# Second attention of a four-layer kernel: values of a key tile formed in one piece instead of two halves

## Chip, core and metric

The kernel runs on one core of a Trainium2 chip. The metric is the device time of one execution in microseconds (us). Engines are named as the profile names them: PE is TensorE (PEld its weight loads), DVE is VectorE, ACT is ScalarE, POOL is GpSimd, SP is SyncE, which issues most DMAs.

## What is computed

Four layers run one after the other on 8192 tokens of 128 channels (16 sequences of 512): a windowed attention, a routed feed-forward layer, a full attention with 16 heads of 8 channels, and a feed-forward layer. Each is wrapped as `x = x + layernorm(layer(layernorm(x)))`. The change lies in the third, whose core in the reference is:

```python
qkv = x @ Wqkv + bqkv
q = _apply_rope(q, cos, sin)
k = _apply_rope(k, cos, sin)
scores = jnp.einsum('bhqd,bhkd->bhqk', q, k) * scale
attn = jax.nn.softmax(scores, axis=-1)
out = jnp.einsum('bhqk,bhkd->bhqd', attn, v)
return out @ Wout + bout
```

No mask is applied: every query of a sequence meets all 512 keys, in each of 16 heads.

## The kernel before

`l1_attention` (L1356) treats one sequence, called a batch here, in 32 **steps** (STEPS). The 16 heads fall into 4 groups (NG) of 4 heads (GH); a group takes 8 steps (UNITS), two steps for each of its 4 key tiles of 128 keys (NT), one for each pair of heads. The batches overlap: while step n of one batch runs, the first half of the next one is prepared 13 steps ahead (AHEAD). Each engine has its own program with the same steps, written out once for two batches inside a loop over batches 2 to 13 (`turns`); batches 0, 1, 14 and 15 stand outside the loop. Every engine works strictly in the order of its program; semaphores tie them together.

In a step, PE issues in this order:

- `shifted` (L1973): two products `d_t_`, the shifted scores of one key tile for one pair of heads, all 512 queries. They go into three banks `t_ps` in turn, so that step n may start once the first of the two exponentials of step n-1 is done.
- `scores` (L1955): two products `d_s_` of a unit 13 steps ahead. DVE takes the row maximum of both (`maximum`, L1759), ACT does the exponentials of `d_t_` into `pT` (L1688).
- what `SLOTS` puts there: the turning in of the normalised tokens (`turn_in`, L1909, step 22 of 32), the four projections of queries and keys (`q0` to `q3`, L1916, steps 23, 24, 26 and 27), the values (`v`, L1921, step 9), the turning out of a finished group (`out0` to `out3`, L1928), `att` (L1935, step 9) and `y` (L1942, step 12). All of them, and `scores`, share the two banks `s_ps` in turn: before each, `room` waits until DVE or ACT has read what stood two places earlier in that order.
- `weighted` (L1986): the product of `pT` of one key tile with the values `v`, added up in the bank `o_ps` (32 partitions for each of the 4 heads, 512 queries) over the four key tiles of a group. Where it stands is told by the table `VALUES`: step within the group's count, key tile, and the halves of the 512 queries.

When a group's last product is done, ACT copies `o_ps` out (L1707, step 10 counted from the group's first), behind its exponentials of that step. The three bf16 parts of queries and keys are made by ACT (L1718, L1722) and POOL and are put into `qs` and `ks` by DMAs that SP issues (L1577). The row maxima go in by four further DMAs for each group (L1585), on the same queue, behind the former where both are due; the first `d_t_` of a group waits for them.

All values are f32 here; a matmul of f32 operands goes to PE as two passes, each an instruction of its own in the trace. The four heads of a product sit on four different column groups of 32 and their passes run side by side, so that 8 instructions (4 heads, 2 passes) form one half of a key tile.

Of the kernel before, what the change touches and what calls it, by code (L numbers as in the profile page):

```python
# [1355 lines left out]
def l1_attention(nc, x, pos, sorted_rows, mean, rstd, wqk_d, wv_d, bqk_d, bv_d, wo_d, bo_d, rope_d, ident_in):  # L1356
# [10 lines left out]
    NT = 4  # L1367
    T = NT * 128
# [4 lines left out]
    GH = 4  # L1373
    NG = H // GH
    HC = 32
# [15 lines left out]
    STACK = {-32: (0, 0, (0, 1, 2)), -31: (1, 0, (0, 3)), -27: (1, 0, (5,)), -26: (0, 1, (3, 4)), -25: (1, 1, (1, 4)),  # L1391
             -24: (0, 2, (5,)), -23: (1, 2, (2,))}
    SHIFTS = -4
    VALUES = ((4, 0, (0, 1)), (5, 1, (0,)), (6, 1, (1,)), (7, 2, (0,)), (8, 2, (1,)), (9, 3, (0,)), (10, 3, (1,)))
    COPY_OUT = 10
    PLUS, ATT = 38, 39
    STAT_Y, STAT_Y2, ROOT_Y, NORM_Y, NORM_Y2, ADD_Y = 47, 48, 51, 60, 62, 63
# [2 lines left out]
    with ExitStack() as ctx:  # L1400
        def sb(name, shape, dt=F32):
            return ctx.enter_context(nc.sbuf_tensor("d_" + name + "_", shape, dt))
# [24 lines left out]
        v = [sb(f"v{k}", [128, NT, H, HC]) for k in range(2)]  # L1427
        nmax = [sb(f"nmax{k}", [128, 32], BF16) for k in range(2)]
        nmaxT = [sb(f"nmaxT{k}", [128, 32], BF16) for k in range(2)]
        pT = [[sb(f"pT{k}_{r}", [128, 2, T]) for r in range(2)] for k in range(NT)]  # L1430
# [24 lines left out]
        o_ps = ps("o", [128, T])  # L1455
# [23 lines left out]
        av_done = sem("av_done")  # L1479
# [43 lines left out]
        for s in range(STAT_IN, STEPS * NB + LAST + 1):  # L1523
            turn = Turn(s // STEPS, 0, 0)
            unit = (s + AHEAD) % STEPS
            for what, at in [(unit, unit - AHEAD)] + [(w, SLOT_STEP[w]) for w in slots_of(s % STEPS)]:
                e = of(turn, s % STEPS, at)
# [21 lines left out]
        def dve_read(what, e):  # L1549

            return counted(what, e, "dve")
# [341 lines left out]
        def _(pe):  # L1893
# [79 lines left out]
                    nc.tensor.matmul(t_ps[(2 * n + a + e.k) % 3][:], ks[e.k][rows, hp, kt * 128:(kt + 1) * 128],  # L1973
                                     qs[e.k][rows, hp, :], start=True, stop=True).then_inc(st_done, 1)

            def weighted(e, g, kt, halves):
                pe.wait_ge(exp_done, 2 * STEPS * e.n + 2 * UNITS * g + 4 * kt + 4)
                if kt == 0:
                    if g == 0:
                        pe.wait_ge(read_dve, dve_read("v", e))  # L1980
                    if not (isinstance(e.n, int) and e.n == 0 and g == 0):
                        pe.wait_ge(oe_done, NG * e.n + g)
                for half in halves:
                    cols = slice(half * T // 2, (half + 1) * T // 2)
                    for i in range(GH):
                        ins = nc.tensor.matmul(o_ps[HC * i:HC * (i + 1), cols], v[e.k][:, kt, g * GH + i, :],  # L1986
                                               pT[kt][i // 2][:, i % 2, cols], start=(kt, half) == (0, 0),
                                               stop=(kt, half) == (NT - 1, 1), skip_group_check=True)
                if halves[-1] == 1:
                    ins.then_inc(av_done, 1)  # L1990

            def step(turn, n):
                e = of(turn, n, n)
                if e is not None:
                    shifted(e, n)
                unit = (n + AHEAD) % STEPS
                e = of(turn, n, unit - AHEAD)
                if e is not None:
                    scores(e, unit)
                for what in slots_of(n):  # L2000
                    e = of(turn, n, SLOT_STEP[what])
                    if e is None:
                        continue
                    room(what, e)
                    if what == "turn_in":
                        turn_in(e)
                    if what[0] == "q":
                        project(e, int(what[1]))
                    if what == "v":
                        project_v(e)  # L2010
                    if what[0:3] == "out":
                        turn_out(e, int(what[3]))
                    if what == "att":
                        turn_attention(e)
                    if what == "y":
                        project_out(e)
                for g in range(NG):
                    for at, kt, halves in VALUES:
                        e = of(turn, n, UNITS * g + at)
                        if e is not None:  # L2020
                            weighted(e, g, kt, halves)

            pe.wait_ge(loaded, 16 * NLOADS)
            pe.wait_ge(const_set, 8)
# [497 lines left out]
```

## Time and profile before

| | us |
|---|---|
| median of 3 runs | 2857.4 |
| lowest and highest run | 2855.66, 2862.07 |
| the profiled execution, device time | 2855.56 |
| its span (first to last instruction) | 2853.8 |
| second attention: first and last `d_t_` of L1973 | 1720.0 to 2644.8 |

The span is 1.8 us shorter than the device time of the same execution. The page of the profile cuts the span into 40 slices of 71 us; the second attention fills slices 25 to 37. In it 512 steps take 925 us, 1.81 us each, and a batch takes 51 to 62 us.

### The profile page before, as it was taken

The page shows a single profiled execution, that of the slowest core. Times are in us where ns is not written, and L with a number is a line of the kernel's source. Part 1 is how long each engine was busy: PE and PEld are TensorE (multiplying, and loading weights), DVE is VectorE, ACT ScalarE, POOL GpSimd, SP SyncE. Part 2 cuts the span into 40 slices and gives each one's busy share as a digit, 9 for nine tenths or more (in the row PEclk, how much of TensorE's full clock was granted, in tenths as well). Part 3 has the DMA queues.
Part 4 walks back from the last instruction along what each step waited for, and adds up shares of the span by engine and source line. Part 5 has one row for each costly group of instructions (what it writes and reads, how often), then busy time and mean ns, then how long its engine had stood idle before and what let it go on. Part 6 is the DMA issues. An engine that isn't in the chain of part 4 may idle for free. (4 is left out here: it accounts for less than half of the span.)

```text
span 2853.8 us, 73730 instructions
## 1 busy us (share of the span) xinstructions
PE 2106.2 (74%) x26748; PEld 1206.3 (42%) x26748; DVE 2078.9 (73%) x5353; ACT 1500.5 (53%) x2776; POOL 1161.3 (41%) x1165
## 2 busy tenths in 40 slices
PE   4898989888989987111009828888888888888597
PEld 3676767666767766100004302222322222232354
DVE  4677777776767775766417828888888888888598
ACT  4565656565656652000005406666666666667487
POOL 5677667676767770000363346311221112210122
PEclk9999999999999996555559958998999999999799
DMA  3233333332333330000022233311122111120001
GB/s 103 65 82 72 73 75 74 79 77 70 74 75 76 75 70 6 1 1 1 21 69 68 77 64 59 51 27 24 24 30 37 28 24 23 29 39 4 9 26 33
DMA packets 103685, 136.76 MB, mean 48 GB/s; under 512 B 23782, under 2 KB 78982, under 8 KB 103047
## 3 DMA queue, kind: packets, MB, share of 16 engines
q1 hardware_dynamic: 99206, 123.34, 19.6%
q0 software_dynamic: 4096, 8.40, 1.1%
q8 instruction: 232, 3.80, 0.6%
q14 instruction: 151, 1.23, 0.2%
HBM read 26.52 MB, written 12.58 MB: 14 GB/s over the span
## 5 line engine op out<-in xcount | busy, mean ns | idle before, releaser
L1759 DVE TENSOR_REDUCE d_nmax_<-d_s_ 128x2 bf16<-128x1024 f32 x512 | 619.9, 1223 | 116.3 <-PE d_s_ L1955 113.7
L1688 ACT ACTIVATE d_pT_<-d_t_ 128x512 f32<-128x512 f32 x1024 | 557.1, 598 | 243.7 <-PE d_t_ L1973 235.7
L303 POOL TENSOR_TENSOR a_other<-a_other,a_rope 128x512 f32<-128x512 f32 x256 | 322.1, 1279 | 300.6 <-DMA a_other<-a_raw 300.4
L1986 PE MATMUL d_o_<-d_pT_,d_v_ 128*32 128x256 f32 x4096 | 332.3, 410 | 0.2 <-ACT d_pT_ L1688 0.2
L1973 PE MATMUL d_t_<-d_qs_,d_ks_ 49*128 49x512 bf16 x1024 | 207.5, 402 | 84.2 <-ACT d_pT_ L1688 42.4
L371 ACT ACTIVATE a_pT<-a_t 64x384 f32<-64x384 f32 x512 | 248.2, 485 | 33.2 <-PE a_t L621 23.9
L509 DVE RECIPROCAL a_rden<-a_o 128x512 f32<-128x512 f32 x64 | 214.5, 3352 | 52.7 <-PE a_o L634 52.7
L1955 PE MATMUL d_s_<-d_ks_,d_qs_ 48*128 48x512 bf16 x1024 | 208.0, 403 | 58.3 <-DMA d_ks_<-d_part_ 29.0
L477 DVE TENSOR_TENSOR a_qT<-a_proj,a_rope 128x512 f32<-128x512 f32 x128 | 87.6, 684 | 165.4 <-ACT a_raw L352 165.3
L1188 ACT ACTIVATE c_hT_<-c_in_,c_beta_,c_gamma_ 128x512 f32<-128x512 f32 x16 | 12.4, 777 | 359.2 <-PE c_in_ L1308 359.2
L823 POOL DMA_INDIRECT sorted_x<-x_tokens,pos x64 | 61.5, 961 | 313.8 <-DVEq L720 294.6
L352 ACT COPY a_raw<-a_proj 128x512 f32<-128x512 f32 x256 | 150.6, 588 | 73.4 <-PE a_proj L540 68.7
L540 PE MATMUL a_proj<-a_xnT_hi,a_w_lo 128*128 128x512 f32 x256 | 116.8, 456 | 93.9 <-ACT a_v L334 88.0
L1973 PEld LDWEIGHTS d_t_<-d_qs_,d_ks_ 49*128 49x128 bf16 x1024 | 49.7, 93 | 316.4 <-ACT d_pT_ L1688 203.5
L358 ACT CAST a_qB<-a_qT 128x512 bf16<-128x512 f32 x128 | 79.3, 620 | 184.9 <-POOL a_qT L308 184.8
L877 PE MATMUL b_tot<-b_count,b_ones 128*128 128x3 bf16 x126 | 23.6, 187 | 201.1 <-DVE b_junk L959 189.3
L643 PE MATMUL a_o<-a_pT,a_v 128*32 128x160 f32 (+1 forms) x4096 | 168.4, 306 | 4.1 <-DVE a_oT L514 2.4
L308 POOL TENSOR_TENSOR a_kT<-a_kT,a_other 128x512 f32<-128x512 f32 x128 | 164.1, 1282 | 0.0
L308 POOL TENSOR_TENSOR a_qT<-a_qT,a_other 128x512 f32<-128x512 f32 x128 | 163.6, 1278 | 0.0
L1986 PEld LDWEIGHTS d_o_<-d_pT_,d_v_ 128*32 128x32 f32 x4096 | 90.5, 111 | 172.6 <-ACT d_pT_ L1688 90.9
L548 PE MATMUL a_y<-a_wo,a_oT 128*128 128x128 f32 x1024 | 135.2, 287 | 17.2 <-issue 16.4
L643 PEld LDWEIGHTS a_o<-a_pT,a_v 128*32 128x32 f32 x4096 | 123.9, 113 | 37.1 <-issue 21.4
(269 smaller groups left out, 4695.6 us busy)
## 6 DMA issues: line engine op xcount, KB each, us to landing
a_other<-a_raw SPq DMA_DIRECT2D x512, 128.0 KB, 2.4
d_qs_<-d_part_ SPq DMA_DIRECT2D x192, 64.0 KB
d_ks_<-d_part_ SPq DMA_DIRECT2D x192, 64.0 KB
a_xpre<-x SPq DMA_DIRECT2D x16, 256.0 KB, 2.8
a_xres<-x SPq DMA_DIRECT2D x16, 256.0 KB, 2.9
c_xs_<-sorted_x SPq DMA_DIRECT2D x16, 256.0 KB, 2.7
c_w_<-e_w SPq DMA_DIRECT2D x16, 256.0 KB, 3.2
sorted_x<-c_xs_ SPq DMA_DIRECT2D x16, 256.0 KB, 2.0
```

The costliest lines, as they stand in the source:

```text
L303: nc.gpsimd.tensor_tensor(other[s % 2][:, side, :], other[s % 2][:, side, :], rope[:, 1, :], ALU.mult).then_inc(rope2_done, 1)
L308: nc.gpsimd.tensor_tensor(dst, dst, other[s % 2][:, side, :], ALU.add).then_inc(add_done, 1)
L352: nc.scalar.copy(raw[s % 2][:, side, :], proj[bank][:, 0:T]).then_inc(copied, 1)
L371: nc.scalar.activation(dst[rows, :, 64 * c:64 * c + HB], src[rows], ACT.Exp, scale=SCALE).then_inc(exp_done, 1)
L509: nc.vector.reciprocal(rden[:], o_ps[:, 0:T]).then_inc(rden_done, 1)
L548: ins = nc.tensor.matmul(y_ps[:, t * 128:(t + 1) * 128], oT[:, 2 * (chunk % 2) + half, t * 128:(t + 1) * 128], wo_sb[:, 2 * chunk + half, ...
L643: ins = nc.tensor.matmul(o_ps[QD * i:QD * (i + 1), 128 * t:128 * t + widths[t]], v_sb[k_v][:, t, col:col + QD], pT[k_p][i][:, BAND * t:BAN ...
L1688: nc.scalar.activation(pT[kt][pair][:, a, :], t_ps[(j + turn.k) % 3][:], ACT.Exp).then_inc(exp_done, 1)
L1759: nc.vector.reduce_max(out, bank_of(unit, e)[:], AX_X, negate=True).then_inc(read_dve, 1)
L1955: nc.tensor.matmul(bank_of(unit, e)[:, a, :], qs[e.k][rows, hp, qt * 128:(qt + 1) * 128], ks[e.k][rows, hp, :], start=True, stop=True).the ...
L1973: nc.tensor.matmul(t_ps[(2 * n + a + e.k) % 3][:], ks[e.k][rows, hp, kt * 128:(kt + 1) * 128], qs[e.k][rows, hp, :], start=True, stop=True ...
L1986: ins = nc.tensor.matmul(o_ps[HC * i:HC * (i + 1), cols], v[e.k][:, kt, g * GH + i, :], pT[kt][i // 2][:, i % 2, cols], start=(kt, half) = ...
```

## The change

The table `VALUES` loses its halves. Before, key tile 0 of a group stood whole in step 4 (both halves, one behind the other), and the two halves of tiles 1, 2 and 3 stood in steps 5 and 6, 7 and 8, 9 and 10. Now tile 0 stands in step 4, tile 1 in step 6, tile 2 in step 8, tile 3 in step 10, each as one product of all 512 queries. `weighted` issues 8 instructions of 512 columns for a key tile where it issued 16 of 256. In the numbering of a batch's 32 steps every even step now has a whole tile and no odd step has any, where before steps 4, 12, 20 and 28 had a whole tile, steps 3, 11, 19 and 27 none, and all others a half.

```diff
-    VALUES = ((4, 0, (0, 1)), (5, 1, (0,)), (6, 1, (1,)), (7, 2, (0,)), (8, 2, (1,)), (9, 3, (0,)), (10, 3, (1,)))
+    VALUES = ((4, 0), (6, 1), (8, 2), (10, 3))
...
-            def weighted(e, g, kt, halves):
+            def weighted(e, g, kt):
...
-                for half in halves:
-                    cols = slice(half * T // 2, (half + 1) * T // 2)
-                    for i in range(GH):
-                        ins = nc.tensor.matmul(o_ps[HC * i:HC * (i + 1), cols], v[e.k][:, kt, g * GH + i, :],
-                                               pT[kt][i // 2][:, i % 2, cols], start=(kt, half) == (0, 0),
-                                               stop=(kt, half) == (NT - 1, 1), skip_group_check=True)
-                if halves[-1] == 1:
-                    ins.then_inc(av_done, 1)
+                for i in range(GH):
+                    ins = nc.tensor.matmul(o_ps[HC * i:HC * (i + 1), :], v[e.k][:, kt, g * GH + i, :],
+                                           pT[kt][i // 2][:, i % 2, :], start=kt == 0, stop=kt == NT - 1)
+                ins.then_inc(av_done, 1)
...
-                    for at, kt, halves in VALUES:
+                    for at, kt in VALUES:
                         e = of(turn, n, UNITS * g + at)
                         if e is not None:
-                            weighted(e, g, kt, halves)
+                            weighted(e, g, kt)
```

The order of PE at the projections, before (from `q0` of step 23 to the values of step 24; in these listings a matmul is one call, so `x2` is two heads; L1973 opens a step). This is the loop's first batch:

```order
L1916 MATMUL d_s_<-d_zT_,d_wqk_ 128x512
L1977 REGISTER_ALU
L1986 MATMUL d_o_<-d_pT_0_,d_v_ 32x256 x2
L1986 MATMUL d_o_<-d_pT_1_,d_v_ 32x256 x2
L1965 REGISTER_ALU
L1973 MATMUL d_t_<-d_qs_,d_ks_ 128x512 x2
L1904 REGISTER_ALU
L1955 MATMUL d_s_<-d_ks_,d_qs_ 128x512 x2
L1904 REGISTER_ALU
L1916 MATMUL d_s_<-d_zT_,d_wqk_ 128x512
L1986 MATMUL d_o_<-d_pT_0_,d_v_ 32x256 x2
L1986 MATMUL d_o_<-d_pT_1_,d_v_ 32x256 x2
```

The same place with the change:

```order
L1916 MATMUL d_s_<-d_zT_,d_wqk_ 128x512
L1965 REGISTER_ALU
L1973 MATMUL d_t_<-d_qs_,d_ks_ 128x512 x2
L1904 REGISTER_ALU
L1955 MATMUL d_s_<-d_ks_,d_qs_ 128x512 x2
L1904 REGISTER_ALU
L1916 MATMUL d_s_<-d_zT_,d_wqk_ 128x512
L1977 REGISTER_ALU
L1984 MATMUL d_o_<-d_pT_0_,d_v_ 32x512 x2
L1984 MATMUL d_o_<-d_pT_1_,d_v_ 32x512 x2
```

Step 23 has lost its half, and step 24 has both halves of the tile in one piece, still behind the projection `q1`.

The order of PE at step 9, with `v` and `att`, and step 10, before:

```order
L1921 MATMUL d_s_<-d_wv_,d_zT_ 128x128 x4
L1904 REGISTER_ALU
L1935 MATMUL d_s_<-d_ident_,d_att_ 128x128 x4
L1977 REGISTER_ALU
L1986 MATMUL d_o_<-d_pT_0_,d_v_ 32x256 x2
L1986 MATMUL d_o_<-d_pT_1_,d_v_ 32x256 x2
L1965 REGISTER_ALU
L1973 MATMUL d_t_<-d_qs_,d_ks_ 128x512 x2
L1904 REGISTER_ALU
L1955 MATMUL d_s_<-d_ks_,d_qs_ 128x512 x2
L1986 MATMUL d_o_<-d_pT_0_,d_v_ 32x256 x2
L1986 MATMUL d_o_<-d_pT_1_,d_v_ 32x256 x2
```

The same place with the change:

```order
L1921 MATMUL d_s_<-d_wv_,d_zT_ 128x128 x4
L1904 REGISTER_ALU
L1935 MATMUL d_s_<-d_ident_,d_att_ 128x128 x4
L1965 REGISTER_ALU
L1973 MATMUL d_t_<-d_qs_,d_ks_ 128x512 x2
L1904 REGISTER_ALU
L1955 MATMUL d_s_<-d_ks_,d_qs_ 128x512 x2
L1977 REGISTER_ALU
L1984 MATMUL d_o_<-d_pT_0_,d_v_ 32x512 x2
L1984 MATMUL d_o_<-d_pT_1_,d_v_ 32x512 x2
```

Here nothing stands between `att` and the next step's `d_t_` and `d_s_` any more; the whole tile has gone behind them.

## Rows read from the trace of the kernel before

**Rows 1.** Page, busy tenths of DVE in 40 slices of 71 us
```profile
DVE  4677777776767775766417828888888888888598
```

**Rows 2.** Windows, whole second attention: window, length, busy us (instructions) by engine, clock
```profile
1720.00:2647.00 927.00, 778.20 (x6836) 265.03 (x6840) 797.18 (x1370) 626.39 (x1175) 211.82 (x194) 0.94 0.19 31
```

**Rows 3.** Waits, 1720 to 2647: engine line, releaser: us, times, longest
```profile
DVE d_nmax_ L1759 <- PE d_s_ L1955: 100.4, 129, 4.4
```

**Rows 4.** Timeline: start, us, engine line op xcount; a half, then a whole tile
```profile
2012.29 0.39 PE L1973 MATMUL d_t_<-d_qs_,d_ks_ 49*128 49x512 bf16 x2
2012.51 0.38 PE L1955 MATMUL d_s_<-d_ks_,d_qs_ 48*128 48x512 bf16 x2
...
2012.71 1.08 ACT L1688 ACTIVATE d_pT_<-d_t_ 128x512 f32<-128x512 f32 x2 [0.63 <-PE d_t_ L1973]
2012.82 0.16 PEld L1986 LDWEIGHTS d_o_<-d_pT_,d_v_ 128*32 128x32 f32 x8 [0.43 <-issue]
2012.82 0.64 PE L1986 MATMUL d_o_<-d_pT_,d_v_ 128*32 128x256 f32 x8
...
2013.39 0.39 PE L1973 MATMUL d_t_<-d_qs_,d_ks_ 49*128 49x512 bf16 x2
...
2081.63 1.07 PE L1986 MATMUL d_o_<-d_pT_,d_v_ 128*32 128x256 f32 x16
...
2082.63 0.39 PE L1973 MATMUL d_t_<-d_qs_,d_ks_ 49*128 49x512 bf16 x2
```

**Rows 5.** Timeline, steps 11 and 12 of batch 6: exponentials and the step they release
```profile
2094.24 2.19 ACT L1688 ACTIVATE d_pT_<-d_t_ 128x512 f32<-128x512 f32 x4
...
2094.92 0.39 PE L1973 MATMUL d_t_<-d_qs_,d_ks_ 49*128 49x512 bf16 x2 [0.83 <-ACT d_pT_ L1688]
```

**Rows 6.** Timeline, steps 22 to 27 of batch 7, PE and DVE
```profile
2173.87 0.65 PE L1909 MATMUL d_s_<-d_ident_,d_zz_ 128*128 128x128 f32 x4 [0.17 <-DVE d_quot_ L1792]
...
2175.02 0.39 PE L1973 MATMUL d_t_<-d_qs_,d_ks_ 49*128 49x512 bf16 x2
...
2175.70 1.23 DVE L1759 TENSOR_REDUCE d_nmax_<-d_s_ 128x2 bf16<-128x1024 f32 x1 [0.69 <-PE d_s_ L1955]
...
2176.84 0.74 DVE L1771 SCALAR_TENSOR_TENSOR d_prod_<-d_s_,d_bqk_,d_rope_ 128x512 f32<-128x512 f32 x1
...
2177.72 1.13 PE L1916 MATMUL d_s_<-d_zT_,d_wqk_ 128*128 128x512 f32 x2
...
2179.35 0.39 PE L1973 MATMUL d_t_<-d_qs_,d_ks_ 49*128 49x512 bf16 x2
...
2180.46 0.39 PE L1973 MATMUL d_t_<-d_qs_,d_ks_ 49*128 49x512 bf16 x2
...
2181.31 1.13 PE L1916 MATMUL d_s_<-d_zT_,d_wqk_ 128*128 128x512 f32 x2 [0.24 <-DVE d_nmax_ L1759]
...
2182.94 0.39 PE L1973 MATMUL d_t_<-d_qs_,d_ks_ 49*128 49x512 bf16 x2
```

**Rows 7.** Timeline, steps 9 and 10 of batch 6, PE and DVE
```profile
2089.70 1.16 PE L1921 MATMUL d_s_<-d_wv_,d_zT_ 128*128 128x128 f32 x8 [1.23 <-DVE d_nmax_ L1759]
...
2091.80 0.64 PE L1986 MATMUL d_o_<-d_pT_,d_v_ 128*32 128x256 f32 x8
...
2093.05 1.23 DVE L1759 TENSOR_REDUCE d_nmax_<-d_s_ 128x2 bf16<-128x1024 f32 x1 [1.30 <-PE d_s_ L1955]
```

**Rows 8.** Timeline, batch 7: DMAs of the maxima, and the step 8 that waits
```profile
2140.48 2.23 SPq L1585 DMA_DIRECT2D d_qs_<-d_nmaxT_  x4
...
2147.00 0.39 PE L1973 MATMUL d_t_<-d_qs_,d_ks_ 49*128 49x512 bf16 x2 [2.92 <-DMA d_qs_<-d_nmaxT_]
```

**Rows 9.** Timeline of PE, steps 0 and 1 of batch 6, after the loop's turn
```profile
2073.80 0.61 PE L1973 MATMUL d_t_<-d_qs_,d_ks_ 49*128 49x512 bf16 x2 [2.43 <-issue]
...
2075.77 0.61 PE L1973 MATMUL d_t_<-d_qs_,d_ks_ 49*128 49x512 bf16 x2
```

**Rows 10.** Windows, batch 6, steps 0 to 2: columns as in Rows 2, clock 0.50
```profile
2073.80:2079.70 5.90, 5.90 (x36) 1.07 (x36) 3.31 (x3) 3.76 (x7) 1.62 (x2) 0.50 0.48 85
```

## The prediction

> **What bounds the kernel now.** I began with the page's 40 slices: the second attention is the long stretch of eights on the vector engine from slice 25 on [rows 1]. The windows give it 797 us of work on the vector engine in 927, against 778 on PE and 626 on ACT [rows 2]. No engine is full. The vector engine has least room, 1.56 us of work in a step of 1.81, and what it waits for is nearly all one thing: the scores of L1955, 100 us in 129 waits [rows 3]. So a change on PE is worth what it does to the time at which `d_s_` comes in those steps where DVE has nothing else. Time saved where DVE is behind is worth nothing, and time added where PE leads DVE costs the full amount. The timeline of single steps, not the sums, decides this.
>
> **Prices of the pieces.** In a step, `d_s_` starts 0.22 us after `d_t_`, the values 0.31 after `d_s_`, and the next `d_t_` 0.57 after a half tile: 1.10 us together [rows 4]. A whole tile in 16 instructions takes 1.00 to the next `d_t_` [rows 4].
>
> The 512-column form in four column groups is not in the trace. Lower bound: the streaming is the same number of columns and each half shows two sets of four passes, so at best only the starts of two sets are saved; I take 0.98. Upper bound: the two passes of `q1`, 512 columns of f32 on all 128 columns with its own weight loads, whose record lasts 1.13 [rows 6] and which holds the next piece off for 1.06 (2179.35 is 1.63 after it starts, less the half's 0.57). I keep 0.98 because the rows of the same product are nearer, and 1.06 for the range.
>
> So a split tile cost 2 x (0.57 + 0.09) = 1.32 us (0.09 is how much later something starts behind `d_s_` when it is the values than when it is the next `d_t_`, 0.31 less 0.22) and a whole one costs 0.98 + 0.09 = 1.07. That is 0.25 saved for each of 3 x 64 = 192 split tiles, 48 us of PE time, and 0.02 for the 64 whole ones, 1 us. What matters is where it lies: an odd step loses 0.57, an even step gains 0.41.
>
> The trace shows all eight weight loads of a half inside 0.16 us while its first passes run [rows 4]. The Trainium skill ("TensorE: Matmul & The Clock Gate", Measured speedup vs the span model) says that weight loads overlap running matmuls only where the row group differs; here all use all 128 rows, so by it each set would stand still for its load, and longer products would save more. The row shows the overlap, and I do not add to the 0.25. The skill's page "TensorEngine Tiling (Array Packing)" (Key Properties) states that changing the tiling mode drains the engine. It speaks for fewer changes between values and scores; what such a change costs is already inside the rows' 0.31 and 0.57, and by it the forecast would stay as it is.
>
> **Light steps do not hand on what they save.** A step may open when the first exponential of the step before is done. The next `d_t_` starts 0.68 after that exponential [rows 5], and an exponential starts 0.42 after its `d_t_` when ACT is idle [rows 4], so two steps lie at least 1.10 us apart however little PE has to do. Before, a pair of steps took 2.2 us on PE and on this chain alike. After, the heavy step takes 0.22 + 0.31 + 0.98 = 1.51 and the light one still 1.10: 2.61. Unless a light step holds other PE work (a slot), its saving is lost, and the 0.41 stays.
>
> **Where DVE covers it: nothing.** In steps 13 to 21 and 4 to 8 the reductions run one behind the other with statistics, quotients and normalisation between them, at 1.5 to 1.7 us a step, and PE waits for room in `s_ps`. Pairs of 2.61 fit below that. If this cover is gone (a stretch where DVE needs less than 1.3 us a step), each pair there costs 0.4.
>
> **Steps 22 to 27, the projections.** Here PE holds most work and DVE waits for it. `turn_in` of step 22 is pinned by DVE's quotients (0.17 wait at 2173.87), so what step 21 saves before it is lost. Then, with [rows 6]:
> - step 22 has the whole tile: step 23 opens at 2173.87 + 0.58 + 0.98 = 2175.43, not 2175.02: +0.41.
> - step 23, light, has `q0`: step 24 opens at 2175.43 + 0.54 + 1.06 = 2177.03, not 2177.18. But the reduction of step 23 is late by 0.41 as well: 2176.11, and the first `d_prod_` follows 1.14 later as before, 2177.25 to 2177.99.
> - step 24: `q1` needs the bank of `q0`, so it waits for that `d_prod_`: 2178.1 where PE would be ready at 2177.57. Step 25 opens at 2178.1 + 1.06 + 0.98 = 2180.13, not 2179.35: +0.78.
> - step 25, light: 1.10 before and after, by the exponential. +0.78 stays.
> - step 26: `q2` waits for the reduction of step 25 as now (0.24), which is late by the same 0.78, then the whole tile: +0.41. Step 27 opens 1.2 late. Steps 27 and 28 are unchanged.
>
> The pattern of these six steps is the same in all batches that have projections, 0 to 13: 14 x 1.2 = **+16.8 us**. From step 28 on DVE is the bound, and carries the delay on.
>
> **Steps 8 to 10.** In step 9, `v` and `att` wait for DVE, and then the half stands before the scores that DVE lacks (1.30 us idle) [rows 7]. It goes: 0.57 earlier. In the five batches that open the loop again this is a full gain, 5 x -0.58 = -2.9. In the nine batches whose step 8 waits for DMAs [rows 8] step 8 starts at the landing and is 0.41 heavier first; where `v` then waits for the vector engine anyway the net is -0.5, where not -0.16. I take -0.35: -3.1. Together **-6.0 us**.
>
> **Steps 30 and 31 and the DMAs behind them.** The scores of step 30 are pinned by DVE, the whole tile behind them makes step 31 and the casts on ACT 0.41 late, and SP's chain of transfers, whose last four carry the maxima of the next group, starts that much later. In nine batches PE's step 8 waits for just these four (2.92 us idle at 2147.00, landing 6.5 after the first issue at 2140.48) [rows 8]. 9 x 0.41 = **+3.7**. Whatever steps 0 to 7 of these batches gain or lose is swallowed by that wait. Where the loop turns, five times, PE stands still about 2.4 us for nothing that the profile shows [rows 9]; the last half before it is gone: 5 x (0.41 - 0.57) = **-0.8**.
>
> **Steps 0 to 3 after the loop's turn.** At the upper clock level steps 0 to 2 go from 1.1 + 1.1 + 1.46 to 1.51 + 1.10 + 1.51, of which DVE feels 0.3. At the lower level of 1.2 GHz (granted clock 0.50 [rows 10]) a step with a half takes 1.97 [rows 9]; a whole tile adds 0.85 (two more sets at twice 0.21), a light step takes 1.33: 2.82 + 1.33 + 2.82 against 5.9, +1.06. Five turns at a mean of 0.7: **+3.5**.
>
> **The last two batches.** There DVE has little to do, and pairs go from 2.2 to 2.6 in some eight pairs: **+3.0**.
>
> **Sum**: 16.8 - 6.0 + 3.7 - 0.8 + 3.5 + 3.0 = +20.2. The profiled execution took 2855.6, so 2875.8; its median is 1.8 higher. I predict 2876.
>
> **Rivals.**
> 1. *PE's saving is on the path.* If light steps are not held by the exponential, or `q1` finds its bank free, the 48 us that PE saves count where DVE waits for it. For: DVE's wait of 100 us is on PE alone. Against: behind a step with no values at all PE still waits 0.83 us for ACT [rows 5]. Half of the 48 us, since DVE is the bound in about half of the steps: 2855.6 - 24 = 2832. It decides as soon as the six projection steps come out shorter than before.
> 2. *All absorbed.* The +0.41 of each heavy step stays within what DVE has queued, also at the projections, and the landing of the maxima is set by something else: only -6 and +6 of small terms, 2857. For: DVE is busy 86%. Against: its 0.69 idle at 2175.70 means that nothing is queued there.
> 3. *More time at the lower clock.* PE works 49 us less and in clumps. The granted clock in the stage is 0.94 [rows 2], and it was at the lower of its two levels behind a stop of 2.4 us [rows 9, 10]. If half of the 64 groups got one heavy step at the lower level (+0.85) and a third of that reached DVE, +9; with 1.06 instead of 0.98 for a whole tile, +0.08 x 3 x 14 = +3.4, and with all turns of the loop slow +1.8: 2890. The Trainium skill ("TensorE: Matmul & The Clock Gate", Why this matters for your kernels) warns of idle gaps between bursts of matmuls, which is the direction of this rival; no row here prices it for light steps.
> 4. *The change is not what it says.* The instruction order shows 8 calls of 32x512 where 16 of 32x256 stood, so no chance is given.
>
> **How the numbers follow.** Forecast 0.6, own range 2864 to 2888; rival 1 0.16; rival 2 0.12; rival 3 0.12. The range reaches over rival 2 and 3 and leaves out most of rival 1: 2853 to 2895. About 0.2% (6 us) is what a measurement of this kernel tells from no change, so "same" is 2852 to 2863. Faster: rival 1, 0.16. Same: rival 2 and a sliver of the forecast, 0.14. Slower 0.70.
>
> **What would show it.** Right: steps 22 to 27 longer by 1.2 us in every batch, with a wait of `q1` for `d_prod_` of about 0.5 that was not there; light steps 1.10 apart; DVE's wait for L1955 up by 10 to 20 us from 100; step 10's reduction 0.5 earlier. PE's busy time down by some 30 to 50 us. Wrong: light steps shorter than 1.0, or whole tiles of more than 1.1 us at the upper clock level, or a time that differs outside 1720 to 2647.

## The result, and the profile after

| | before | after |
|---|---|---|
| median, us | 2859.74 | 2869.62 |
| lowest and highest | 2853.06, 2862.80 | 2864.93, 2872.48 |
| ratio, 95% interval | | 1.0035 [1.0019, 1.0051] |
| profiled execution: device time | 2855.56 | 2868.84 |
| its span | 2853.8 | 2867.0 |
| second attention, first to last `d_t_` | 924.4 | 932.0 |

The change makes the kernel slower by 9.9 us, where 16 to 19 were forecast (2876 beside medians of 2857 to 2860). The two profiled executions differ by more, 13.3 us. The second attention holds 7.6 of that. 8.1 us had already gathered by the end of the first attention, whose code is the same, and the stages between and behind gave 2.4 of them back. The experiments come back to it.

The page after. Each line of engines has busy us, share, instructions; the groups have busy us and mean ns of one, then the idle time before them:

```profile
PE 2069.4 (72%) x24700; PEld 1152.6 (40%) x24700; DVE 2081.6 (73%) x5353; ACT 1501.0 (52%) x2776; POOL 1160.9 (40%) x1165
...
DVE  4677777776767775777417828888898888988598
...
q8 instruction: 176, 2.88, 0.4%
...
L1759 DVE TENSOR_REDUCE d_nmax_<-d_s_ 128x2 bf16<-128x1024 f32 x512 | 621.5, 1224 | 122.4 <-PE d_s_ L1955 105.9
...
L1984 PE MATMUL d_o_<-d_pT_,d_v_ 128*32 128x512 f32 x2048 | 282.3, 624 | 0.2 <-ACT d_pT_ L1688 0.2
```

The vector engine's row is that of [rows 1] but for single tenths. PE's total was 2106.2 before: the change does save 37 us of PE. The window of the whole stage, which answers to [rows 2], and three waits in it, which answer to [rows 3]:

```profile
1727.00:2663.00 936.00, 734.15 (x4792) 205.71 (x4792) 799.51 (x1371) 627.67 (x1176) 211.29 (x194) 0.96 0.19 29
```

```profile
DVE d_nmax_ L1759 <- PE d_s_ L1955: 92.9, 107, 2.4
...
DVE d_nmax_ L1759 <- issue: 13.4, 7, 4.4
...
ACT d_oE_ L1707 <- PE d_o_ L1984: 30.3, 38, 1.6
```

PE is busy 44 us less in the stage, and the granted clock went up from 0.94 to 0.96, which rival 3 had the other way round. The vector engine waits for `d_s_` 7.5 us less, not 10 to 20 more. The other two waits grew: the reductions' idle time for which no releaser is shown (`issue`) from 0.3 us to 13.4, and ACT's copy of `o_ps` out from 21.3 to 30.3.

**Where the time went.** Both traces have 512 reductions L1759 in the same order, so each can be set against its partner. This table adds up by how much the second kernel falls behind (+) or gains (-) between the reductions of two steps. It is worked out from the two timelines, batches 0 to 13 together, with the forecast's terms beside it:

| reductions, step to step | after less before, us | forecast |
|---|---|---|
| 31 to 0 (loop's turn) | -2.1 | -0.8 |
| 0 to 4 | -3.7 (five batches behind the turn: -7.8) | +3.5 |
| 4 to 7 | +2.2 | 0 |
| 7 to 9 | +11.5 | +3.7, and part of -6.0 |
| 9 to 10 | -12.0 | rest of -6.0 |
| 12 to 13 | -6.2 (the same five batches: -6.3) | 0 |
| 10 to 12 and 13 to 21 | -1.2 | 0 |
| 21 to 27 (projections) | **+16.7** | **+16.8** |
| 27 to 31 | -0.7 | 0 |
| batches 14 and 15, all steps | +2.0 | +3.0 |
| sum | +6.5 | +26.2 - 6.0 = +20.2 |

Read by batch (from step 31 of the batch before to its own step 31), the same comparison says where the cost stays. Batches 0 to 3 fall behind by 5.3 us and 14 and 15 by 2.4, while the ten batches 4 to 13 come out even (-0.4). There each batch that follows a turn of the loop gains 1.2 to 3.4 us, and its successor loses 1.5 to 3.3. The second execution of the changed kernel, set against the same one of before, gives +7.9, +3.7 and -0.2. So the projections' 1.2 us is paid in every batch, but inside the loop something else pays it back.

### The profile page after: what moved, and what is told of

Read it like the earlier page. It is cut to its first block and busy times, and to the rows that moved or that the text cites. A ratio compares the mean times of both kernels' runs of the same rounds, so it can differ in the third digit from the quotient of the medians.

```text
span 2867.0 us, 69628 instructions
## 1 busy us (share of the span) xinstructions
PE 2069.4 (72%) x24700; PEld 1152.6 (40%) x24700; DVE 2081.6 (73%) x5353; ACT 1501.0 (52%) x2776; POOL 1160.9 (40%) x1165
## 5 line engine op out<-in xcount | busy, mean ns | idle before, releaser
L1759 DVE TENSOR_REDUCE d_nmax_<-d_s_ 128x2 bf16<-128x1024 f32 x512 | 621.5, 1224 | 122.4 <-PE d_s_ L1955 105.9
L1973 PE MATMUL d_t_<-d_qs_,d_ks_ 49*128 49x512 bf16 x1024 | 205.3, 397 | 112.6 <-ACT d_pT_ L1688 84.0
L1984 PE MATMUL d_o_<-d_pT_,d_v_ 128*32 128x512 f32 x2048 | 282.3, 624 | 0.2 <-ACT d_pT_ L1688 0.2
L1973 PEld LDWEIGHTS d_t_<-d_qs_,d_ks_ 49*128 49x128 bf16 x1024 | 49.6, 93 | 443.9 <-ACT d_pT_ L1688 317.0
L548 PEld LDWEIGHTS a_y<-a_wo,a_oT 128*128 128x128 f32 x1024 | 125.8, 200 | 31.7 <-issue 30.6
```

The costliest lines, as they stand in the source:

```text
L548: ins = nc.tensor.matmul(y_ps[:, t * 128:(t + 1) * 128], oT[:, 2 * (chunk % 2) + half, t * 128:(t + 1) * 128], wo_sb[:, 2 * chunk + half, ...
L1759: nc.vector.reduce_max(out, bank_of(unit, e)[:], AX_X, negate=True).then_inc(read_dve, 1)
L1984: ins = nc.tensor.matmul(o_ps[HC * i:HC * (i + 1), :], v[e.k][:, kt, g * GH + i, :], pT[kt][i // 2][:, i % 2, :], start=kt == 0, stop=kt = ...
```

## The projections as the forecast has them

The timeline of batch 7, steps 22 to 27, answers to [rows 6]: start, us, engine, line, operation, and the idle time before it in brackets.

```profile
2184.61 0.65 PE L1909 MATMUL d_s_<-d_ident_,d_zz_ 128*128 128x128 f32 x4 [0.17 <-DVE d_quot_ L1792]
...
2186.19 0.39 PE L1973 MATMUL d_t_<-d_qs_,d_ks_ 49*128 49x512 bf16 x2
...
2187.79 0.39 PE L1973 MATMUL d_t_<-d_qs_,d_ks_ 49*128 49x512 bf16 x2
...
2188.80 1.12 PE L1916 MATMUL d_s_<-d_zT_,d_wqk_ 128*128 128x512 f32 x2 [0.26 <-DVE d_prod_ L1771]
...
2190.86 0.39 PE L1973 MATMUL d_t_<-d_qs_,d_ks_ 49*128 49x512 bf16 x2
...
2191.93 0.39 PE L1973 MATMUL d_t_<-d_qs_,d_ks_ 49*128 49x512 bf16 x2 [0.47 <-ACT d_pT_ L1688]
...
2193.88 1.06 PE L1984 MATMUL d_o_<-d_pT_,d_v_ 128*32 128x512 f32 x8
...
2194.87 0.39 PE L1973 MATMUL d_t_<-d_qs_,d_ks_ 49*128 49x512 bf16 x2
```

From `turn_in` to the opening of step 27 it is 10.26 us, where it was 9.07: +1.19. The wait of `q1` for `d_prod_` that was forecast as about 0.5 is there (0.26 on PE, and its weights waited 0.56). A whole tile holds the next `d_t_` off for 0.99 to 1.00 (2193.88 to 2194.87), where 0.98 was taken. The light step 25 is 1.07 long and PE waits for ACT at its end, where 1.10 was taken.

## Is the 13 us between the profiled executions all the change's?

```diff
(no edit: the kernel before, and the changed kernel, once more)
```

> The kernel before, profiled once more. The changed kernel's profile began its second attention 7.3 us later than the profile of before, in code that neither differs in. Theory A (that is drift between executions): here the first attention, which ended at 1103 us in the profile of before and at 1111 us in that of the change, ends anywhere between these two, and the stretch of the second attention from the first to the last shifted scores takes 925 us within 1 us. Theory B (the changed kernel's code slows the first stages too): the first attention ends at 1103 within 1 us.

> The changed kernel, profiled once more. Theory A (drift): the first attention ends more than 1 us away from the 1111 us of the first profile, and the second attention has again a length 7 to 8 us above that of before. Theory B (its code): the first attention ends at 1111 within 1 us.

The kernel before took 2860.03, the changed one 2871.53. The first attention ended at 1103.0 and 1108.6 us in two executions of the kernel before, and at 1111.1 and 1103.9 in two of the changed kernel. So this unchanged stretch moves by up to 8.1 us from one execution to the next, in both kernels. The theory that the change's shorter code shifts it falls. In the second attention the lengths are 924.4 and 925.0 before, 932.0 and 937.5 after, so the second profile of the changed kernel is 12.5 us above before, not the 7 to 8 that theory A named with the drift. The medians, +9.9, lie between the two.

Paired with the first execution of before as in the table above, its second gave +0.6 in all and a third, on a further chip (below), +0.4. Single cells moved by more: 12 to 13 by +3.0 and +1.3, 9 to 10 by +0.8 and -2.1, 0 to 4 by -2.1 and +0.8, 21 to 27 by 0.0 and +1.1. The two executions of the changed kernel differ by 4.1 in all, 3.1 of it between steps 13 and 21 of batch 0. That is the noise of these tables: a cell of 3 us tells nothing alone, the +16.7, +11.5, -12.0 and -6.2 are clear of it.

## Place or form: two halves behind each other in the changed places

```diff
-    VALUES = ((4, 0, (0, 1)), (5, 1, (0,)), (6, 1, (1,)), (7, 2, (0,)), ...
+    VALUES = (((4, 0, (0, 1)), (6, 1, (0, 1)), (8, 2, (0, 1)), (10, 3, (0, 1))), ...   # in all four groups
```

> Whole tiles in steps 4, 6, 8 and 10 as in the change, but each still as two halves of 256 queries one behind the other: placement without the new form, and as many instructions of PE as before. Theory A (a whole tile costs 0.02 less than two halves; the branch of PE's program at the loop's turn took 3.5 us before and 0.2 after because the loop's code became shorter): the branch takes 3.5 us again at all five turns, steps behind the turn are at the lower clock level again, and the time is 5 to 15 us above that of the change, some 15 to 25 above before, which is what the blind sum of 20 had assumed. Theory B (the short branch came from where PE stands when it branches, not from the length of its code): the branch stays short and the time is that of the change within 4 us.

Measured: 2889.1 (2880.3 to 2898.2), ratio 1.0097 [1.0065, 1.0129], 29 us beside a kernel before of 2860.0. The projections' steps 24 to 27 lose 16 us here as in the changed kernel, and steps 9 to 13 gain the same. What is new lies at the loop's turn: in the five batches behind it 8.9 us between steps 31 and 0 and 5.4 between 0 and 4, where the changed kernel gains. So the *place* costs, and the *form* of 512 columns gives back some 19 us by the medians (26 in the two profiled executions, of which this kernel's was the slowest of its four), most of it at the turn. The branch is long as theory A has it, but longer than its 3.5 us, and the time lies above its 5 to 15. The trace says where: PE's branch at the turn (L1501) takes 3.4 to 4.0 us before, 4.8 to 5.4 here and 0.2 in the changed kernel. It is short in every kernel here with 176 or 178 packets of instructions on queue 8, and long in every one with 226 or 232. The traces show that these go together. They don't show how the length of the code would make the branch long. The timeline of PE in this kernel shows what stands behind the branch in one turn:

```profile
2091.85 0.61 PE L1979 MATMUL d_t_<-d_qs_,d_ks_ 49*128 49x512 bf16 x2 [4.31 <-issue]
...
2094.68 0.61 PE L1979 MATMUL d_t_<-d_qs_,d_ks_ 49*128 49x512 bf16 x2
```

It stands still for 4.31 us, then runs step 0 at the lower clock level, 2.83 us long. And the changed kernel, one batch pair:

```profile
2084.70 0.39 PE L1973 MATMUL d_t_<-d_qs_,d_ks_ 49*128 49x512 bf16 x2 [0.96 <-ACT d_pT_ L1688]
...
2086.81 1.23 DVE L1759 TENSOR_REDUCE d_nmax_<-d_s_ 128x2 bf16<-128x1024 f32 x1 [1.66 <-issue]
```

```profile
2084.70:2089.40 4.70, 3.84 (x28) 0.81 (x28) 3.04 (x4) 4.08 (x8) 2.23 (x2) 1.00 0.30 57
```

PE waits 0.96, for ACT, where [rows 9] had 2.43 for nothing shown, and goes on at a granted clock of 1.00, where [rows 10] had 0.50. But the vector engine has a turn of its own, 1.66 us of nothing, and now it is the one that comes last: of the 1.5 us that PE gains, the reductions gain 0.4 at the turn itself. The larger gain is the clock's, -7.8 in steps 0 to 4 where +3.5 was forecast.

## The projections, from both sides

Group 2 alone back in halves (steps 20 to 26 as before), all else as in the change:

```diff
-        ((4, 0, WHOLE_TILE), (6, 1, WHOLE_TILE), (8, 2, WHOLE_TILE), (10, 3, WHOLE_TILE)),   # group 2
+        ((4, 0, (0, 1)), (5, 1, (0,)), (6, 1, (1,)), (7, 2, (0,)), (8, 2, (1,)), (9, 3, (0,)), (10, 3, (1,))),
```

> The change, but group 2 (steps 20 to 26, where the four projections stand) has its halves in the old places. Theory A (the steps 22 to 27 cost 1.2 us in each of 14 batches and that is carried on): 16 to 17 us below the change, 2853 beside 2870 and 2860, faster than before by 5 to 8 us. Theory B (the delay at the projections is given back at the next wait for a DMA or at the loop's turn): less than 8 us below the change.

Measured: 2865.8, ratio 1.0018 [1.0000, 1.0036] to a kernel before of 2860.0: 6 us below the one execution of the changed kernel on that chip, not 17. That is theory B's size, and its interval overlaps the changed kernel's. In the trace the projection steps 24 to 27 stand at 0.0 in all batches, so the local price is confirmed in full. But 6.1 us have come between steps 27 and 31 (4.9 of them in the odd batches 5 to 13), 3.1 between 21 and 24, and the gain in steps 0 to 4 behind the turn is 4.7 instead of 7.8.

The opposite kernel, halves everywhere and group 2 alone whole:

```diff
-        ((4, 0, (0, 1)), (5, 1, (0,)), (6, 1, (1,)), (7, 2, (0,)), (8, 2, (1,)), (9, 3, (0,)), (10, 3, (1,))),   # group 2
+        ((4, 0, WHOLE_TILE), (6, 1, WHOLE_TILE), (8, 2, WHOLE_TILE), (10, 3, WHOLE_TILE)),
```

> The kernel before, with group 2 alone (steps 20, 22, 24 and 26) in whole tiles; groups 0, 1 and 3 keep their halves. Theory A (the projection steps 22 to 27 cost 1.2 us a batch wherever the rest of the table stands): 14 x 1.2 = 16.8 us more than the kernel before, 2877, and the reductions between step 21 and step 27 late by 1.2 us in every batch from 0 to 13. Theory B (vector engine or clock give it back, as when group 2 alone was put back into halves and only some 5 us of the change's time went): 5 us, 2865. If PE's branch at the loop's turn is short here, some 2 us less in either case; if it is long, the loop's code still counts as long.

It ran on a chip on which the kernel before took 2903.3: there the first two batches lose some 35 us in each of the four kernels traced, with two stops of ACT of 10 to 17 us and shorter ones of the vector engine of up to 14. Only ratios and batches 4 to 13 are used from it. Measured: 2922.4, ratio 1.0073 [1.0050, 1.0096], +19.1 us. In the ten batches 4 to 13 steps 24 to 27 lose 11.3 us, 1.13 each, and 21 to 24 another 3.1. Theory A: here almost nothing gives it back (+13.4 in all over these batches).

Then the same four tiles whole, but not behind `q1` and `q2`:

```diff
-        ((4, 0, WHOLE_TILE), (6, 1, WHOLE_TILE), (8, 2, WHOLE_TILE), (10, 3, WHOLE_TILE)),   # group 2
+        ((4, 0, WHOLE_TILE), (5, 1, WHOLE_TILE), (7, 2, WHOLE_TILE), (9, 3, WHOLE_TILE)),
```

> The kernel before, with group 2 alone in whole tiles, but at steps 20, 21, 23 and 25: none in the steps 22, 24 and 26. Theory A (it is the place of the whole tile that costs: behind q0, q1 and q2 in step 24 and 26): steps 22, 24 and 26 are lighter by a half each, q1 finds its bank free, and steps 22 to 27 become shorter by about 0.9 us in each of 14 batches: 12.5 us below the kernel before, 2847. Theory B (whole tiles cost at the projections wherever they stand, since a pair of steps gets 2.61 instead of 2.2 us): as group 2 whole in even steps, 2865 to 2877.

Measured on the same chip: 2911.6, ratio 1.0024 [1.0007, 1.0040], +8.3. The move is worth 10.8 us against group 2 whole in the even steps, and in batches 4 to 13 the traces put 11.9 of it into steps 21 to 27. The time itself lies at the lower edge of theory B's range (ratio 1.002 to 1.006), so neither theory holds as it stands: the place counts, but a whole tile costs at the new place too. My working of -12.5 against the kernel before was wrong: steps 24 to 27 do gain (0.39 a batch), but the whole tile of step 21 costs 0.63 between 21 and 24 first.

## Step 8, and the clock behind a stop

The changed kernel, batch 7, from the last `d_t_` ahead of the wait for the maxima's DMAs on; it answers to [rows 8]:

```profile
2152.94 0.39 PE L1973 MATMUL d_t_<-d_qs_,d_ks_ 49*128 49x512 bf16 x2
...
2156.75 0.61 PE L1973 MATMUL d_t_<-d_qs_,d_ks_ 49*128 49x512 bf16 x2 [3.20 <-DMA d_qs_<-d_nmaxT_]
...
2157.72 1.93 PE L1984 MATMUL d_o_<-d_pT_,d_v_ 128*32 128x512 f32 x8
...
2159.58 0.61 PE L1973 MATMUL d_t_<-d_qs_,d_ks_ 49*128 49x512 bf16 x2
...
2160.68 1.23 DVE L1759 TENSOR_REDUCE d_nmax_<-d_s_ 128x2 bf16<-128x1024 f32 x1 [1.21 <-PE d_s_ L1955]
```

The windows of what follows the stop (the column ahead of the DMA share is the granted clock), after:

```profile
2156.70:2163.10 6.40, 6.35 (x30) 2.93 (x30) 3.29 (x5) 2.17 (x4) 0.00 (x0) 0.54 0.51 102
```

and in the kernel before, whose step 8 was over in 1.11 us:

```profile
2147.00:2152.30 5.30, 5.30 (x36) 3.17 (x36) 3.46 (x5) 2.61 (x5) 0.00 (x0) 0.68 0.51 103
```

The stop is 0.3 us longer than before (3.20 and 2.92), and behind it the whole step 8 runs at the lower level of 1.2 GHz. It takes 2.83 us, where 1.51 was priced. The vector engine has nothing else and waits 1.21 us for the scores of step 9. Its reductions are late by 0.5 at step 8 and by a further 1.3 at step 9. Of these the 0.5 answers to the forecast's 0.41 for the landing, the 1.3 to a term that I had at 0.41 and then netted away. To see whether it is this tile in this place:

```diff
-        ((4, 0, WHOLE_TILE), (6, 1, WHOLE_TILE), (8, 2, WHOLE_TILE), (10, 3, WHOLE_TILE)),   # group 0
+        ((4, 0, WHOLE_TILE), (6, 1, WHOLE_TILE), (7, 2, WHOLE_TILE), (10, 3, WHOLE_TILE)),
```

> The changed kernel, with tile 2 of group 0 alone moved from step 8 to step 7, ahead of the wait for the maxima's DMAs. Theory A (the whole tile behind that stop is run at the lower clock level and costs 0.9 to 1.4 us in each of nine batches, since nothing but PE holds the vector engine there): 9 to 12 us below the change, 2859 to 2862, step 8 about 1.1 to 1.3 us long instead of 2.8, step 7 longer inside the wait. Theory B (the vector engine has enough queued after the stop, or v waits for it anyway): within 3 us of the change, 2868 to 2874.

Measured: 2905.2, ratio 1.0008 [0.9995, 1.0020], so 8 us below the change by the ratios, the two on different chips, where theory A had 9 to 12 and theory B 3 at most. The same step 8 there:

```profile
2195.28 1.06 PE L1991 MATMUL d_o_<-d_pT_,d_v_ 128*32 128x512 f32 x8
...
2198.26 0.39 PE L1979 MATMUL d_t_<-d_qs_,d_ks_ 49*128 49x512 bf16 x2 [1.91 <-DMA d_qs_<-d_nmaxT_]
...
2199.33 0.39 PE L1979 MATMUL d_t_<-d_qs_,d_ks_ 49*128 49x512 bf16 x2 [0.46 <-ACT d_pT_ L1694]
```

```profile
2198.20:2203.80 5.60, 4.44 (x32) 2.05 (x32) 4.14 (x6) 3.54 (x7) 0.00 (x0) 1.00 0.47 104
```

The tile is done inside the wait, the stop shrinks to 1.91, step 8 takes 1.07 at a granted clock of 1.00. Batch 7 is the best case. In batches 9, 11 and 13 step 8 is at the upper level too, but step 9 has a mean granted clock of 0.62 to 0.65, and in batch 5 both steps are at 0.50. Even so the light step 8 takes only 1.29 there, so most of the gain comes from the tile being gone and not from a better clock.

In the five odd batches 5 to 13 steps 7 to 9 lose 0.3 us instead of 8.8. That is theory A in its place, and the largest single thing that the forecast had left out. Here too something comes back: 5.8 us between steps 21 and 24 of those batches (0.3 in the change). Over batches 4 to 13 this trace is only 2.1 us ahead of the change's, so the 8 us of the ratios are not found in full.

## What gives part of each gain back

A last pair of single edits, with a trace of the kernel before from the same chip:

> The kernel before once more, for a trace of it from the chip on which the next three run. On another chip the whole of it took 2903 us instead of 2857 to 2860, and the readings of three variants put 34 to 36 us of that into steps 4 to 8 of the first batches (0 and 1). If this chip is like that one, these steps are some 34 us longer here too, which is then the chip's and not the edit's; if it is like the first, the second attention takes 924 to 926 us.

It took 2860.23, with a second attention of 924.8 us like that of the first trace: the 35 us of the other chip are that chip's.

```diff
-        ((4, 0, (0, 1)), (5, 1, (0,)), (6, 1, (1,)), (7, 2, (0,)), (8, 2, (1,)), (9, 3, (0,)), (10, 3, (1,))),   # group 0 of before
+        ((4, 0, WHOLE_TILE), (6, 1, WHOLE_TILE), (7, 2, WHOLE_TILE), (10, 3, WHOLE_TILE)),
```

> The kernel before, with group 0 alone in whole tiles, at steps 4, 6, 7 and 10 (none in step 8, which may wait for DMAs, and none in step 9, behind att). Theory A (a half behind att in step 9 delays the scores of step 10 by 0.57 in nearly all batches): step 10's reduction 0.6 to 0.8 earlier in 14 batches, -8 to -11, and nothing at step 12, whose 1.26 us in five batches belongs to group 1: 0.3 to 0.4% below the kernel before. Theory B (the gain at step 12 comes with it, since PE is then at the upper clock level when step 12 begins): -14 to -17, 0.5 to 0.6% below. PE's branch at the loop's turn long, 3.4 to 3.9 us, in both.

Measured: 2846.5, ratio 0.9951 [0.9934, 0.9968], 12.7 us faster. Against the trace of before from the same chip, steps 9 to 10 gain 7.4 us and step 12 another 7.4 (9.4 and 6.1 against the first trace). So the gain at step 12 comes with it as in theory B, whose total of 14 to 17 is not reached. In the kernel before PE is at the lower level in part of step 12 in four or five of the five batches behind a turn, in each of its three traces, after group 0's change in none. The window of step 12 of batch 6, before:

```profile
2095.40:2100.30 4.90, 3.96 (x28) 2.14 (x28) 3.13 (x5) 1.03 (x2) 0.86 (x1) 0.65 0.14 17
```

The branch is long, 3.3 to 3.9 us. 9.2 us come back between steps 21 and 24 of batches 1, 5, 11 and 13. The profiled execution is the slowest of the eight, 2858.1, and its second attention only 2.8 us shorter than that of before. So the trace shows where gains and losses lie, and not how the other executions come to 12.7.

```diff
-        ((4, 0, WHOLE_TILE), (6, 1, WHOLE_TILE), (8, 2, WHOLE_TILE), (10, 3, WHOLE_TILE)),   # group 2 of the change
+        ((4, 0, WHOLE_TILE), (5, 1, WHOLE_TILE), (7, 2, WHOLE_TILE), (9, 3, WHOLE_TILE)),
```

> The changed kernel, with group 2 alone at steps 20, 21, 23 and 25 instead of 20, 22, 24 and 26. Theory A (whole tiles behind q1 and q2 are what costs at the projections, and their place alone mends it): steps 21 to 27 about 1.1 us shorter in each of 14 batches, 15 us below the change, some 5 us below the kernel before (ratio 0.998). Theory B (as with group 2 alone put back into halves, most of the local gain is given back elsewhere): 6 us below the change, ratio 1.002.

Measured: 2863.4, ratio 1.0022 [1.0009, 1.0035]: theory B. Its interval overlaps the change's, so that it is faster at all isn't settled. In the trace, again of the slowest of its executions, steps 24 to 27 are 21 us better than in the change, and 27 to 31 are 9.8 worse, 21 to 24 4.9, 0 to 4 behind the turn 3.4, and the whole stage is 2.3 us longer than in the first trace of the change. The place is step 30, batch 5. First this kernel (L1979 is `shifted`, L1991 `weighted`):

```profile
2079.32 0.39 PE L1961 MATMUL d_s_<-d_ks_,d_qs_ 48*128 48x512 bf16 x2 [1.54 <-DVE d_nmax_ L1765]
...
2079.64 1.80 PE L1991 MATMUL d_o_<-d_pT_,d_v_ 128*32 128x512 f32 x8
...
2081.38 0.61 PE L1979 MATMUL d_t_<-d_qs_,d_ks_ 49*128 49x512 bf16 x2
...
2084.12 1.93 PE L1991 MATMUL d_o_<-d_pT_,d_v_ 128*32 128x512 f32 x8
```

```profile
2077.38:2081.30 3.92, 2.38 (x13) 0.35 (x12) 3.85 (x7) 1.97 (x4) 1.81 (x2) 0.81 0.00 0
2081.37:2085.90 4.53, 3.78 (x20) 0.54 (x16) 1.65 (x3) 2.67 (x5) 1.16 (x1) 0.50 0.09 23
```

and the changed kernel:

```profile
2081.82 0.39 PE L1955 MATMUL d_s_<-d_ks_,d_qs_ 48*128 48x512 bf16 x2 [1.50 <-DVE d_nmax_ L1759]
...
2082.14 1.06 PE L1984 MATMUL d_o_<-d_pT_,d_v_ 128*32 128x512 f32 x8
...
2083.14 0.39 PE L1973 MATMUL d_t_<-d_qs_,d_ks_ 49*128 49x512 bf16 x2
```

```profile
2079.92:2083.10 3.18, 1.68 (x13) 0.35 (x12) 3.11 (x5) 1.97 (x4) 1.71 (x2) 1.00 0.00 0
2083.13:2086.20 3.07, 2.11 (x20) 0.47 (x16) 2.02 (x4) 2.64 (x5) 1.02 (x2) 1.00 0.01 3
```

The order of work is the same in both from step 27 on, and so is the stop of PE (1.54 and 1.50 us, for room in `s_ps`). Behind it the one falls to the lower clock level inside the whole tile and stays there through step 0, the other doesn't. From step 30 to step 1 it is 8.6 us against 6.3. Group 2 in halves shows the same (8.5 us, clock 0.83, then 0.50).

Counting the steps whose `d_t_` record is long (0.61 us, lower level, not 0.39) gives this, of 512, with the steps in which they lie in batches 4 to 13:

| kernel | steps at the lower level | most of them in steps |
|---|---|---|
| before (three traces) | 36, 36, 41 | 0 to 3, 13, 21 |
| after (two traces) | 26, 27 | 8 and 9 only |
| placed halves | 41 | 0 to 5, 8, 9 |
| group 2 in halves | 44 | 31, 0, 1, 8, 9 |
| change, group 2 odd | 42 | 31, 0, 1, 8, 9 |
| group 0 alone | 48 | 0 to 3, 10, 23 |

On the chip with the long first batches it was 48 (group 2 whole), 55 (group 2 odd) and 36 (tile 2 in step 7).

So the lower clock moves when single places are mended, and takes part of what they give. That it takes it is shown: 8.5 of the 9.8 us between steps 27 and 31 lie in the six batches whose step 31 is at the lower level. Why it falls in the one kernel and not in the other behind equal stops isn't. What differs between the kernels is the work ahead of step 27, and no run here isolates that. The table alone doesn't decide it either: in batch 7 of this same kernel the stop is 1.55 us and the clock stays at 1.00.

## Whole tiles where nothing waits behind them

The readings name the bad places: behind `q1` and `q2` (24, 26), behind the DMAs' stop (8), and step 30, where PE stops for room. The table that avoids them (the move of group 1 from steps 16 and 18 to 15 and 17 answers to none of these, and no run isolates it):

```diff
-    VALUES = ((4, 0), (6, 1), (8, 2), (10, 3))
+    VALUES = (((4, 0), (6, 1), (7, 2), (10, 3)),
+              ((4, 0), (6, 1), (7, 2), (9, 3)),
+              ((4, 0), (5, 1), (7, 2), (9, 3)),
+              ((4, 0), (5, 1), (7, 2), (9, 3)))      # one row a group
```

> Whole tiles in all groups as in the change, but at places chosen by the readings: group 0 in steps 4, 6, 7, 10; group 1 in 12, 14, 15, 17; group 2 in 20, 21, 23, 25; group 3 in 28, 29, 31 and 1 of the next batch. Theory A (whole tiles save PE time and cost only where they stand behind a projection or behind the wait for DMAs): change 2871, less 16.8 and a further 12.5 at group 2, less 9 at step 8, with step 9 as in the change: 2834. Theory B (the vector engine is the bound as soon as PE's costs at these places go, and the two lie in the same stretch of its queue): not below 2852.

> Whole tiles at steps 4, 6, 7, 10; 12, 14, 15, 17; 20, 21, 23, 25; 28, 29, 31 and 1, once more, on the chip of these runs. On the other chip it was at 0.988 of the kernel before. If that comes from the table and not from the chip: 0.987 to 0.990 here too, 2823 to 2832 beside a kernel before of 2860; if it comes from that chip's long first batches, 0.991 to 0.995.

Measured on the slow first-batch chip: 2870.3 beside 2903.3, ratio 0.9881 [0.9863, 0.9899]. On the chip of the last runs: 2831.7 (2823.8 to 2834.5) beside 2859.2, ratio 0.9908 [0.9881, 0.9934], **27 us faster than before and some 37 faster than the change**. The first run is theory A (2834 beside 2860 is 0.991), with more gained than it had. The second leaves open how much of the 33 us on the first chip was that chip's: 2831.7 lies inside the range given for the table alone, the ratio 0.9908 between the two ranges, and its interval reaches into both. No run has this table with the tiles as halves, so what the shorter code at the loop's turn adds to the 27 us isn't told apart.

The trace of the second run, paired with the first trace of before, batches 0 to 13: steps 21 to 27 +1.5 (change +16.7), 7 to 9 -7.1 (+11.5), 31 to 0 -9.6 (-2.1), 0 to 4 -8.2 (-3.7), 9 to 10 -11.8, 12 to 13 -6.2, against that 27 to 31 +7.6 and 4 to 7 +4.6. The place of step 30, batch 5:

```profile
2060.95 1.06 PE L1991 MATMUL d_o_<-d_pT_,d_v_ 128*32 128x512 f32 x8
...
2062.89 0.39 PE L1961 MATMUL d_s_<-d_ks_,d_qs_ 48*128 48x512 bf16 x2 [0.55 <-DVE d_nmax_ L1765]
...
2066.87 1.23 DVE L1765 TENSOR_REDUCE d_nmax_<-d_s_ 128x2 bf16<-128x1024 f32 x1 [0.19 <-issue]
```

```profile
2061.95:2065.00 3.05, 2.26 (x20) 0.54 (x16) 2.98 (x5) 2.63 (x6) 0.96 (x1) 1.00 0.01 3
2065.00:2069.10 4.10, 2.92 (x20) 0.74 (x20) 3.91 (x5) 3.71 (x8) 2.29 (x3) 1.00 0.22 50
```

The tile now stands ahead of PE's stop, in step 29, and shortens it from 1.5 us to 0.55. From step 30 to step 1 it is 4.1 us (6.3 in the change, 7.8 before). The scores of step 31 come so early that the vector engine has work queued when its program turns, and it idles 0.19 us there instead of 1.66; with it goes the -9.6 between steps 31 and 0. Of 512 steps 23 are at the lower level. The vector engine's wait for the scores is 70.5 us in this kernel, 100 before [rows 3].

## Why the forecast was right in direction and too large

- **The projections, +16.8: right, by their own steps**, measured +16.7. They decide the direction, and nothing of rival 1 or 2 shows there: light steps are 1.07 apart, `q1` waits.
- **Prices of the pieces: right** (whole tile 1.00 for 0.98, light step 1.07 for 1.10, heavy 1.53 for 1.51). Eight instructions of 512 columns hold the next `d_t_` off as long as sixteen of 256 (0.99 to 1.00 and 1.00), so in a whole tile the longer form itself saves next to nothing. The sentence of the Trainium skill on weight loads that the prediction draws on stands in the section "The mechanism" of "TensorE: Matmul & The Clock Gate", just above the one named.
- **Steps 8 to 10, -6.0 in the sum: mis-sized on both sides.** Step 9's gain was larger, -12.0 instead of 14 x 0.58 = 8.1 at most. Step 8's cost was larger still: in eight of the nine batches that wait for DMAs the whole tile runs at the lower clock (in batch 2, behind a stop of 1.44, it doesn't), +1.3 where I had +0.41 before netting. I had priced this very thing, 2.82 us for a heavy step at that level, but only for the loop's turn. I did not ask it of a stop of 2.92 us that was in my own rows. The landing of the maxima, +3.7 by 0.41 a batch, measured 0.5.
- **The loop's turn, -0.8 and +3.5: wrong sign.** The step that failed is that the forecast kept PE's stop of 2.4 us and the lower clock behind it, without giving a reason. The stop was the branch, and it fell to 0.2 us. With it went the lower clock in steps 0 to 3: -3.7 (-7.8 in the five batches behind a turn) and -2.1 in place of +2.7.
- **Step 12, -6.2: missed.** It needed the granted clock of that step in the kernel before, which I had not read.
- **The last two batches, +3.0: +2.0.**
- **Of the signs to look for**, PE's busy time (-37 for -30 to -50), light steps and the wait of `q1` came as said. The vector engine's wait for scores went down by 7.5, not up, since the clock's gains count in the same sum. Rival 3 had the mechanism (the clock decides some us) with the wrong direction for the change itself. It showed its face in the single edits. One sign of being wrong did appear: 5.7 us of the profiled pair lie outside the second attention. It was drift between executions, as the repeats show.
- **The total is in part luck.** Outside the projections the terms were forecast at +3.4 and came to -10.2. The error is mostly the turn with the clock behind it (-8.5) and step 12 (-6.2), while those at step 8 and step 9 nearly cancel (+1.8). The mechanism at the projections was right; the waits and the clock around them were carried over from the kernel before.

## What to carry to other kernels

Ask of longer instructions first where they stand. In this kernel a heavy piece did well ahead of a wait that was there anyway, and badly behind it or behind work whose buffer the next engine frees: the same instructions cost 10 us in one set of places and gain 27 in another. The form counts too, 19 us in the same places, most of it at the loop's turn. After every stop (here the clock fell behind some of 1.5 us) look at the granted clock of the next step in both kernels, and price the work there at the level found.

## What was not expected of the hardware

- PE's branch at the loop's turn took 0.2 us in kernels with 176 or 178 instruction packets, 3.3 to 4.0 us with 226 or 232, and 4.8 to 5.4 in the one with two halves in each heavy step, which has 232 too. So the count of packets goes with it, but isn't all, and no run shows the cause. The vector engine's turn, whose code is the same in all of them, stops it for 1.66 us in the change and for 0.19 us in the last kernel, where work lay queued ahead of it.
- The clock can fall or stay behind stops of the same length (1.50 and 1.54 us, above); the clock stays in all five turns of the change, and falls in four of the five of the other kernel. In the kernel before it is the same at the turn: behind stops of 2.5 us it is at the lower level in step 0 of batch 4, behind 2.75 it isn't in step 0 of batch 8.
- An unchanged stretch of 1.1 ms moved by up to 8 us between executions, and one chip took 44 us more for the same program, mostly in its first two batches of this stage, with stops of ACT of 10 to 17 us. A difference of 10 us in one profiled pair is no evidence; a paired table of one stage is, for cells of more than some 3 us.
